# A four-layer graph kernel: the upper triangle by row pairs, seven products per four units

## What is computed

```python
h = jnp.maximum(_layernorm(x, axis=-1), 0.0)
x = x + _L0_gnn_ref(h, adj, L0_gnn_u)            # adj @ dropout(h)
h = jnp.maximum(_layernorm(x, axis=-1), 0.0)
x = x + _L1_gnn_ref(h, adj, L1_gnn_W, L1_gnn_b)  # (adj @ h + h) / deg, concat, W, relu, L2 norm
h = jnp.maximum(_layernorm(x, axis=-1), 0.0)
x = x + _L2_gnn_ref(h, adj, L2_gnn_W)            # D^-1/2 (adj + I) D^-1/2 h W
h = jnp.maximum(_layernorm(x, axis=-1), 0.0)
x = x + _L3_gnn_ref(h, adj, L3_gnn_W)            # adj @ h / (deg + 1), concat, W
```

## Time and profile before

| | us |
|---|---|
| median of 3 runs | 1928.79 (1928.42 to 1930.34) |
| profiled execution, device time | 1928.06 |
| its span, first to last instruction | 1926.1 |
| upper stage, main part (L579 begins, phase 3 begins) | 799.8 to 1192.6 |

### The profile page before, as it was taken

How to read it: one execution, slowest core, us unless ns; L and a number is a source line. 1 busy time by engine, 2 the same in 40 slices (tenths; PEclk the granted TensorE clock), 3 DMA queues, 4 the chain that set the end, 5 groups by cost and what they waited for, 6 DMA issues and landing times.

```text
span 1926.1 us, 17779 instructions
## 1 busy us (share of the span) xinstructions
PE 1884.6 (98%) x7160; PEld 732.9 (38%) x7160; DVE 870.9 (45%) x1030; ACT 115.3 (6%) x293; POOL 3.3 (0%) x18
## 2 busy tenths in 40 slices
PE   5899999999999999999999999999999999999998
PEld 1233333333333333444444444344444444344333
DVE  8988899999887762622121111321111100110332
ACT  0000000000000001100000000111100000000000
POOL 0000000000000000000000000000000000000000
PEclk9999999999999999999999999999999999999999
DMA  9999999999988884598888887497999889999998
GB/s 386 421 421 421 421 421 422 421 421 412 352 328 319 303 297 172 237 355 286 300 286 303 289 300 262 186 400 287 399 377 374 339 307 422 369 371 410 361 422 342
DMA packets 95167, 670.29 MB, mean 348 GB/s; under 512 B 11120, under 2 KB 13168, under 8 KB 14192
## 3 DMA queue, kind: packets, MB, share of 16 engines
q1 hardware_dynamic: 92160, 666.94, 87.9%
q10 hardware_dynamic: 2928, 2.23, 0.3%
HBM read 667.03 MB, written 2.10 MB: 347 GB/s over the span
## 4 chain that ended last, share of the span: by engine, by line
PE 87%; DMA 7%; DVE 5%; issue 0%; ACT 0%; SPq 0%; DVEq 0%
PE acc L549 44%; PE acc L579 36%; DMA ring<-stream_in 7%; PE Z L600 3%; PE HT L549 2%; PE DEG L611 1%; PE HT L643 1%; PE DEG L620 0%; DVE z_sb L934 0%; DVE states L942 0%; DVE x L983 0%; DVE z_sb L981 0%; DVE centred L899 0%; DVE squares L901 0%; DVE mean L898 0%
## 5 line engine op out<-in xcount | busy, mean ns | idle before, releaser
L549 PE MATMUL acc<-ring,states 128*64 128x512 f32 x3992 | 894.3, 596 | 32.6 <-DMA ring<-stream_in 27.8
L579 PE MATMUL acc<-ring,states 128*128 128x512 f32 x1792 | 778.8, 593 | 0.0
L549 PEld LDWEIGHTS acc<-ring,states 128*64 128x64 f32 x3992 | 281.7, 137 | 584.9 <-issue 554.2
L579 PEld LDWEIGHTS acc<-ring,states 128*128 128x128 f32 x1792 | 336.7, 190 | 414.5 <-issue 414.5
L1000 DVE TENSOR_TENSOR row_sum<-row_sum,ring 128x2048 f32<-128x2048 f32 x194 | 444.6, 2292 | 18.6 <-DMA ring<-stream_in 13.6
L934 DVE TENSOR_TENSOR z_sb<-Z,deg_rsqrt 128x256 f32<-128x256 f32 x16 | 6.8, 424 | 335.3 <-PE Z L600 335.3
L967 DVE TENSOR_TENSOR y<-acc,y 64x512 f32<-64x512 f32 x16 | 11.1, 692 | 282.3 <-PE acc L579 274.9
L549 PE MATMUL acc<-diag,states 128*64 128x512 f32 x432 | 103.6, 595 | 0.5 <-DMA diag<-stream_in 0.5
L406 ACT COPY y<-acc 64x512 f32<-64x512 f32 x44 | 25.5, 581 | 1014.2 <-PE acc L549 739.4
L600 PEld LDWEIGHTS Z<-below,y 128*128 128x128 f32 x512 | 62.9, 191 | 50.6 <-issue 15.8
L1061 DVE TENSOR_TENSOR y<-acc,y 64x512 f32<-64x512 f32 x36 | 24.6, 682 | 110.3 <-PE acc L549 110.0
(11 more groups left out here) (84 smaller groups left out, 383.7 us busy)
## 6 DMA issues: line engine op xcount, KB each, us to landing
ring<-stream_in SPq DMA_DIRECT2D x604, 1024.0 KB, 9.8
diag<-stream_in SPq DMA_DIRECT2D x28, 1024.0 KB, 11.4
x<-x_in SPq DMA_DIRECT2D x4, 512.0 KB, 7.2
y<-u_in SPq DMA_DIRECT2D x4, 512.0 KB, 9.2
x_out<-x ACTq DMA_DIRECT2D x16, 128.0 KB, 7.4
below<-w_in ACTq DMA_DIRECT2D x6, 16.0 KB, 5.8
bias<-b_in ACTq DMA_DIRECT2D x1, 32.0 KB, 9.9
```

The source lines that it names most:

```text
L549: return nc.tensor.matmul(half_of(bank, half), h[layer % 2][:, J], moving, start=start, stop=stop)
L579: done = nc.tensor.matmul(acc[bank][:, :], states[:, J * 2 * F:(J + 1) * 2 * F], source_tile(slot(key), k), start=first and k == 0, stop=l ...
```

## The change

Rows 10 to 1 of the upper stage are taken in five pairs of rows, `PAIRS`, and their sources in pairs too, where all four units lie above the diagonal: 17 **fours**, of 2, 3, 4, 4 and 4 in the five row pairs. With the two rows hi and lo, the sources s1 and s2 and the states of both layers this is a product of 2 x 2 blocks, and it is made from seven 64-wide products P1 to P7 (Winograd's form of Strassen) where eight were. P1 to P7 need four sums of units, which VectorE forms, partly in place in the ring (`first_form`, `third_form`, `last_forms`), and four differences of states per source pair (`formed`, in the `diag` buffers; two source pairs on GpSimd, two on VectorE). TensorE takes two products at a time. An even four issues four groups, and the fourth has the P1 of the next four beside P3; an odd four issues three. Where no next four is there (row pair (8, 7)), P3 runs alone.

What isn't in a four: the unit (lo, hi) next to the diagonal (`near`), whose layer 2 part needs row hi's new states. It is loaded a second time (`"again"`) and multiplied beside the next pair's `near` (`behind`). Eleven sources remain for both rows (`plain_both`, 22 units). Row 0's 15 units stay at full width (`cover`), and are dealt out over the row pairs. At the end of a row pair VectorE adds its banks up (`combine_...`), bank by bank, and each bank is awaited alone by the next pair's first products (`pair_taken`).

In groups of four pairs of matmuls, each as long as one unit at full width: 15 covers, 60 groups for the fours, 22 plain, 6 near and behind, 103 in all.

```diff
+PAIRS = [(10, 9), (8, 7), (6, 5), (4, 3), (2, 1)]
+SOURCE_PAIRS = [(15, 14), (13, 12), (11, 10), (9, 8)]
+FOURS = [[sp for sp in SOURCE_PAIRS if sp[1] > hi] for hi, lo in PAIRS]
...
+PLAIN = [list(range(min(s for sp in FOURS[p] for s in sp) - 1, PAIRS[p][0], -1)) for p in range(len(PAIRS))]
+PAIR_STEPS = [
+    [("cover", 15), ("cover", 14), ("four", 0), ("near", 0), ("four", 1), ("plain", 11)],
+    [("cover", 13), ("four", 0), ("four", 1), ("near", 1), ("four", 2), ("cover", 12), ("plain", 9)],
+    [("cover", 11), ("four", 0), ("four", 1), ("near", 2), ("four", 2), ("four", 3), ("cover", 10), ("plain", 7)],
+    [("cover", 9), ("cover", 8), ("four", 0), ("four", 1), ("near", 3), ("four", 2), ("plain", 7), ("plain", 6),
+     ("four", 3), ("plain", 5)],
+    [("cover", 7), ("four", 0), ("four", 1), ("near", 4), ("four", 2), ("plain", 7), ("plain", 6), ("four", 3),
+     ("plain", 5), ("plain", 4), ("plain", 3)],
+]
+COVER_AT_END = [6, 5, 4, 3, 2, 1]
...
+        s1, s2 = FOURS[p][n]
+        return [(2, lo, s1), (2, lo, s2), (2, hi, s1), (2, hi, s2)]
+    if kind == "near":
+        return ([("again", *PAIRS[p - 1][::-1])] if p else []) + [(2, lo, hi)]
+    return [(2, hi, n), (2, lo, n)]
...
-BANK_UP = {13: 0, 12: 2, 11: 4, 14: 3, 10: 1}
-for b in range(9, -1, -1):
-    BANK_UP[b] = BANK_UP[b + 5]
+BANK_UP = {13: 0, 12: 2, 11: 4, 14: 3, 0: 1}
+GATHERS = {"P2": (0, 0), "P1": (0, 1), "P5": (2, 0), "P4": (2, 1), "P7": (4, 0), "P6": (4, 1),
+           "P1 again": (3, 0), "P3": (3, 1), "plain": (5, 0), "behind": (5, 0)}
...
+            gp.wait_ge(*diag_let_go(1, LAST))
+            for n, (s1, s2) in enumerate(SOURCE_PAIRS[:FORMED_BY_GPSIMD]):
+                gp.wait_ge(*state(2, s2))
...
+                nc.gpsimd.tensor_tensor(t1, b12, b11, ALU.subtract).then_inc(gp_step, 1)
+                nc.gpsimd.tensor_tensor(t3, b22, b12, ALU.subtract).then_inc(gp_step, 1)
...
+                act.wait_ge(*pair_done(p))
+                if p > 0:
+                    act.wait_ge(pair_taken, 3 * p)
+                nc.scalar.copy(pair_sum(0), product("P1")).then_inc(p1_copied, 1)
...
+            def four_even(p, i, after_first=None, after_second=None):
+                (hi, lo), (s1, s2) = PAIRS[p], FOURS[p][i]
+                n, last = FOURS_BEFORE[p] + i, i == len(FOURS[p]) - 1
+                a11, a12, a21, a22 = [(2, b, g) for b in (hi, lo) for g in (s1, s2)]
+                await_unit(a12, 1)
+                await_unit(a11, 1)
+                for k in range(TPR):
+                    two = nc.tensor.matmul(product("P2"), h[1][:, s2 * TPR + k], source_tile(slot(a12), k),
+                                           start=i == 0 and k == 0, stop=False)
+                    one = nc.tensor.matmul(product("P1"), h[1][:, s1 * TPR + k], source_tile(slot(a11), k),
+                                           start=i == 0 and k == 0, stop=i >= len(FOURS[p]) - 2 and k == TPR - 1)
+                two.then_inc(second_taken, 1)
+                one.then_inc(first_taken, 1)
+                if after_first is not None:
+                    after_first()
+                if i == 0 and p > 0:
+                    pe.wait_ge(pair_taken, 3 * p - 2)
+                pe.wait_ge(*states_formed_of((s1, s2)))
+                pe.wait_ge(unit_formed, 4 * n + 1)
+                await_unit(a22, 2)
+                for k in range(TPR):
+                    five = nc.tensor.matmul(product("P5"), formed((s1, s2), 1)[:, k], source_tile(first_sum[n % 2], k),
+                                            start=i == 0 and k == 0, stop=last and k == TPR - 1)
+                    four = nc.tensor.matmul(product("P4"), formed((s1, s2), 4)[:, k], source_tile(slot(a22), k),
+                                            start=i == 0 and k == 0, stop=False)
+                five.then_inc(sum_taken, 1)
+                four.then_inc(unit_freed, 1)
+                if after_second is not None:
+                    after_second()
+                pe.wait_ge(unit_formed, 4 * n + 3)
+                for k in range(TPR):
+                    seven = nc.tensor.matmul(product("P7"), formed((s1, s2), 3)[:, k], source_tile(slot(a21), k),
+                                             start=i == 0 and k == 0, stop=last and k == TPR - 1)
+                    nc.tensor.matmul(product("P6"), formed((s1, s2), 2)[:, k], source_tile(slot(a11), k),
+                                     start=i == 0 and k == 0, stop=last and k == TPR - 1)
+                seven.then_inc(unit_freed, 1)
+                pe.wait_ge(unit_formed, 4 * n + 4)
+                if i == 0 and p > 0:
+                    pe.wait_ge(pair_taken, 3 * p - 1)
+                if not last:
+                    t1, t2 = FOURS[p][i + 1]
+                    await_unit((2, hi, t1), 1)
+                for k in range(TPR):
+                    if not last:
+                        one = nc.tensor.matmul(product("P1 again"), h[1][:, t1 * TPR + k],
+                                               source_tile(slot((2, hi, t1)), k), start=i == 0 and k == 0,
+                                               stop=i >= len(FOURS[p]) - 3 and k == TPR - 1)
+                    three = nc.tensor.matmul(product("P3"), h[0][:, s2 * TPR + k], source_tile(slot(a12), k),
+                                             start=i == 0 and k == 0, stop=False)
+                if not last:
+                    one.then_inc(first_taken, 1)
+                three.then_inc(unit_freed, 2)
+            def four_odd(p, i):
...
+                two.then_inc(second_taken, 1)
+                pe.wait_ge(unit_formed, 4 * n + 3)
...
+                if p > 0:
+                    before_hi, before_lo = PAIRS[p - 1]
+                    await_unit(("again", before_lo, before_hi), 2)
+                    pe.wait_ge(pair_taken, 3 * p)
+                for k in range(TPR):
+                    if p > 0:
+                        behind = nc.tensor.matmul(product("behind"), h[0][:, before_hi * TPR + k],
+                                                  source_tile(slot(("again", before_lo, before_hi)), k),
+                                                  start=k == 0, stop=k == TPR - 1)
+                    near = nc.tensor.matmul(product("P4"), h[1][:, hi * TPR + k], source_tile(slot((2, lo, hi)), k),
...
+            pe.wait_ge(*gathered(1, LAST))
+            for p, (hi, lo) in enumerate(PAIRS):
+                for kind, n in PAIR_STEPS[p]:
+                    if kind == "cover":
+                        cover(n)
+                        if p > 0 and n == PAIR_STEPS[p][0][1]:
+                            finish(1, PAIRS[p - 1][0])
+                    elif kind == "four" and n == 0:
+                        if p == 0:
+                            pe.wait_ge(*gathered(1, 11))
+                            pe.wait_ge(part_copied, PARTS.index((2, 11)) + 1)
+                        four_even(p, 0, after_first=(lambda: finish(1, PAIRS[p - 1][1])) if p else None,
+                                  after_second=lambda: turn_own(1, hi))
+                        turn_own(1, lo)
+                    elif kind == "four" and n % 2 == 0:
+                        four_even(p, n)
+                        if p == len(PAIRS) - 1:
+                            turn_own(1, 0)
+                    elif kind == "four":
+                        four_odd(p, n)
+                    elif kind == "near":
+                        near_diagonal(p)
+                    else:
+                        plain_both(p, n)
...
+            def first_form(p, i):
+                (hi, lo), (s1, s2) = PAIRS[p], FOURS[p][i]
+                n = FOURS_BEFORE[p] + i
+                a21, a22 = (2, lo, s1), (2, lo, s2)
+                dve.wait_ge(*loaded(a21))
+                dve.wait_ge(*loaded(a22))
+                if n >= 2:
+                    dve.wait_ge(*fours_taken(n - 2))
+                nc.vector.tensor_tensor(first_sum[n % 2][:, :], slot(a21)[:, :], slot(a22)[:, :],
+                                        ALU.add).then_inc(unit_formed, 1)
+                dve.wait_ge(unit_formed, 4 * n + 1)
+            def third_form(p, i):
+                (hi, lo), (s1, s2) = PAIRS[p], FOURS[p][i]
+                n = FOURS_BEFORE[p] + i
+                a11, a21 = (2, hi, s1), (2, lo, s1)
+                dve.wait_ge(*loaded(a11))
+                nc.vector.tensor_tensor(slot(a21)[:, :], slot(a11)[:, :], slot(a21)[:, :],
+                                        ALU.subtract).then_inc(unit_formed, 1)
+                dve.wait_ge(unit_formed, 4 * n + 2)
+            def last_forms(p, i):
+                (hi, lo), (s1, s2) = PAIRS[p], FOURS[p][i]
+                n = FOURS_BEFORE[p] + i
+                a11, a12 = (2, hi, s1), (2, hi, s2)
+                dve.wait_ge(first_taken, n + 1)
+                nc.vector.tensor_tensor(slot(a11)[:, :], first_sum[n % 2][:, :], slot(a11)[:, :],
+                                        ALU.subtract).then_inc(unit_formed, 1)
```

(64 more changed lines are left out.)

225 lines of the change are left out of this document (191 added, 34 removed).

## The result

| | before | changed |
|---|---|---|
| median of 20 runs each, us | 1929.73 (1927.63 to 1931.73) | 1932.54 (1926.79 to 1935.53) |
| profiled execution, device time | 1928.06 | 1933.26 |
| its span | 1926.1 | 1931.4 |
| upper stage, main part | 392.8 | 397.2 |
| mean granted clock of TensorE | 1.000 | 0.996 |

The ratio is 1.0014 (95% interval 1.0007 to 1.002): slower by 0.14%, which is inside the 0.2% that I had called no change, and 8.4 us above my forecast of 1924.1, outside the range. I had forecast 4.7 us less than before, and it is 2.8 more; the other 0.9 is the level of the kernel before, 1929.73 over 20 runs where the forecast started from 1928.8 over three. The runs of the changed kernel lie 8.7 us apart, those of before 4.1. That spread is the first sign: nothing in the sum varies from run to run.

A forecast was written before the change was run, and what follows sets the result against it. TensorE was taken to bound the upper stage (busy 391.5 of 392.8 us). 372.2 without waits + 15.3 waits + 0.4 GpSimd = 387.9 against 392.6, -4.7 us: forecast 1924.1 us, range 1916.5 to 1931.

The forecast's parts named there:

- The shift of the products: Upper stage: TensorE's 103 groups take 354.1 us, 23.6 less than 377.7; forms add 157 us on VectorE, inside its 322.
- the sum without waits: Upper stage: products, `finish`, transpositions and changes between full width and pairs add up to 372.2 us, 20.4 less than before.
- VectorE becomes the bound: Rival, in every four: forms beyond 3.3 us delay TensorE; at 4.0 us each, 17.5 us more, 1941.6; chance 0.12.
- no effect: Rival: lone and mixed pairs run one after another, the stage longer by whole groups (60 x 3.4 us); excluded, no chance given.
- The lone half: Three groups with half the array idle, priced like a pair; one overlap, behind the first `near`, gives -0.9 us.
- The waits, 15.3: Upper stage: TensorE waits for VectorE at three row-pair starts (6.3), four `near` (5.9), source 5 (1.9), plus 8 x 0.15 us.
- The price of a wait: Each wait of TensorE for VectorE counted at its length plus a 0.15 us lag; at row-pair starts 2.1, 6.3 for three.
- GpSimd, 0.4: Ahead of the upper stage: GpSimd's state operations hold up VectorE's chain for rows 15 and 14 by 0.4 us, bounds 0 to 2.1.
- Loads: Upper stage: five more units loaded, all hidden; tightest in row pairs (4, 3) and (2, 1), third four, 0.8 us to spare.
- Thin margins: Rival: two of late loads, GpSimd beside VectorE and odd-four forms miss by a microsecond a row pair: 1928 to 1932; chance 0.14.
- Fewer waits: Rival: TensorE's 15.3 us of waits for VectorE shrink; half gone gives 1916.5, all gone 1908.8; chance 0.18.

The follow-up runs named there:

- both orders: Changed kernel; VectorE forms two sums ahead of adding up the old row pair's banks and begins `end_layer_1` ahead of the odd four's `last_forms`: 1912.96 us.
- the first order: Changed kernel; VectorE forms the first and third sum of a row pair's first four ahead of adding up the old pair's banks: 1920.94 us.
- the second order: Changed kernel; VectorE begins the rest of `end_layer_1` ahead of the odd four's `last_forms`, row hi in four 1, row lo in four 3: 1922.81 us.
- the third of the stalled ones: Kernel before, without seven products; TensorE made to wait for one VectorE operation of 128x2048, eight times in the upper stage: 1958.30 us.
- the longest stall: Kernel before, without seven products; TensorE made to wait for two VectorE operations of 128x2048, eight times in the upper stage: 1986.05 us.

## Why the prediction was wrong

- **The shift of the products: right.** Full-width forms take 2.292 us on VectorE as in the earlier trace rows, now 17 times at L1285:

```profile
L1285 DVE TENSOR_TENSOR ring<-ring 128x2048 f32<-128x2048 f32 x17 | 39.0, 2292 | 42.6 <-PE acc L883 42.3
```

  The kernel with both orders has almost no waits, and its stage shows the sum without waits: 375.7 less 1.6 is 374.1, against 372.2. The rival in which VectorE becomes the bound didn't happen, and "no effect" is excluded by the same 374.1.
- **The lone half, -0.9: wrong.** The first `near` does run ahead on its half, but the other half then ends last: from its start at 822.15 to the cover at 842.90 are 20.75 us for six groups, 6 x 3.438 = 20.63. Nothing is gained. It is half of the 1.9 us that the sum was short; no row shows the other half.
- **The waits, 15.3: right in place and number, 1.4 short (16.7).** At L852 2.1 + 0.15 were forecast, 0.4 + 1.9 measured; at L915 1.65 against 1.87, at L931 2.05 against 2.18.
- **The price of a wait: the step that failed.** "It waits 2.1, 6.3 us for three" counted a wait at its own length. Behind four of the eight stood a stretch at half clock of 1.7 us: 6.8 us in the profiled execution, about three of them, 5.1, in the median run (1932.5 against 1927.4 for runs without). The waits of the earlier trace rows gave no warning, since at 0.79 and 0.89 us they are of the length behind which no run here shows a low clock; and the kernel before has no wait in the stage. With 5.1 + 1.4 + 0.9 = 7.4 the change would have been forecast at +2.7 instead of -4.7; it measured +2.8. The three stretches of the median run are an estimate from its time, since only one execution has a trace. The remaining 0.9 of the 8.4 is the level of the kernel before, as said.
- **GpSimd, 0.4: too low by 0.4 in the rows.** VectorE's chain ahead of the stage was 0.8 us longer. The stage began 0.5 us later than before, but that start is no measure of it: in the kernels with the same head it lies anywhere between 800.32 and 802.09. The rule that the prediction quoted from the Trainium skill (SBUF — State Buffer, Who interferes with whom) holds here: the two operations with two SBUF inputs beside GpSimd's reading were stretched, the reduction with one was not. GpSimd's operations took 0.72 to 0.91 us, not the 0.56 estimated by scaling from the Trainium skill's GPSIMD Engine Reference (Elementwise), and not the 0.52 of the memset.
- **Loads: right here, and thin as said.** No wait for them in the changed kernel; with its delays gone, two of 0.8 us appear. (The 14.6 us on record was added up from 4.6, where the row says 4.8; with that the margin is 0.6 us.)
- **The rivals.** "Thin margins" had the size of the miss and the wrong cause. "Fewer waits" named the lever: half of them gone was priced at 7.7 us; the first order took 7.0 us of waits and gave 11.0 (8.2 under the kernel before beside it, where the changed kernel is 2.8 above).

## What to carry to other kernels

Where TensorE has been at full clock without a break, price a new wait of 2 us at its length plus 1.7 us times the chance that the clock falls behind it (here 11 of 24 over all traces, from 0 of 8 at one line to 2 of 2 at another), and look at the clock column rather than at busy time, which hides it. A spread between runs that the kernel before didn't have is the quickest sign. Waits that can't be removed can be filled with products that add nothing (3.7 us here, each kernel against the one before beside it), but letting the slower engine do the awaited form first was worth 11.0, and both orders 19.0.

## What the runs showed of the hardware

- Behind a wait of 1.9 to 2.4 us TensorE ran at half clock in 11 of 24 cases (4 of 8 in the changed kernel, 1 of 5 in the first order, 1 of 3 in the second, 5 of 8 in the third of the stalled ones), with the record pair at 0.85 us instead of 0.43; behind 0.65 and 1.32 us in 0 of 16, behind 4.7 in 8 of 8.
- The low clock can begin with the first product behind the wait (1.12 us at 859.77 in the second order, and the window from 866.08 in the longest stall) or after it (0.64 us at 858.43 in the changed kernel, 1.06 at 859.66).
- A `TENSOR_TENSOR` of 128 x 256 on GpSimd took 0.72 to 0.91 us, and stretched an operation of VectorE with two SBUF inputs from 0.42 to 0.70 and 0.83.
- A half of the array that started a group early gave nothing back where the other half wasn't ahead too: 20.75 us for six groups, 6 x 3.438 = 20.63.
